# Attention megakernel: weighted sums taken two key tiles at a time, and the buffers regrouped for it

## The reference

```python
def ffn(x):                       # per sequence, N = 8 adapters, rank 64
    base = x @ W_base + b_base
    h = relu(x @ W_enc[n] + b_enc[n])                 # all n
    losses = mean((h @ W_dec[n] + b_dec[n] - x) ** 2) # one number per n
    a = connected_idx[argmin(losses)]
    return base + relu(x @ W_down[a] + b_down[a]) @ W_up[a] + b_up[a]

def attn(x):                      # 16 heads of 16, rotary q and k
    q, k, v = rope(x @ Wq + bq), rope(x @ Wk + bk), x @ Wv + bv
    return concat(softmax(q @ k.T / 4) @ v) @ W0 + b0

x = x + 0.5 * ffn(layernorm(x))
x = x + attn(layernorm(x))
x = x + 0.5 * ffn(layernorm(x))
```

## Time and profile before

| | before |
|---|---|
| time, median of 3 runs | 1844.04 us (1842.85 to 1847.05) |
| profiled execution: time, span of its instructions | 1842.72 us, 1840.9 us |
| PE busy | 1739.8 us, 95% |
| DVE busy | 1286.3 us, 70% |
| ACT busy | 978.3 us, 53% |
| POOL busy | 497.6 us, 27% |
| chain of work that ended last | PE 81%, DVE 11%, ACT 2%, DMA 2% |
| granted TensorE clock, mean | 0.976 of full speed |

### The profile page before, as it was taken

The page is one execution under the profiler, slowest core; times in us unless marked ns, Lnnn a source line. Parts: engine busy times, 40 slices in busy tenths (PEclk is TensorE's granted clock), DMA queues, the critical chain, the costliest instruction groups (busy, mean ns, idle before and its releaser), DMA issues.

```text
span 1840.9 us, 26466 instructions
## 1 busy us (share of the span) xinstructions
PE 1739.8 (95%) x9128; PEld 987.3 (54%) x9128; DVE 1286.3 (70%) x2795; ACT 978.3 (53%) x1954; POOL 497.6 (27%) x665
## 2 busy tenths in 40 slices
PE   6478999999999999999999999999999999999976
PEld 4343555555555555555556555555556555554434
DVE  5459686867768676776868677686867768686521
ACT  1126465655646565564646556474655637465531
POOL 2415041231414123141413214050322405032101
PEclk9689999999999999999999999999999999999996
DMA  4334231233333123333322333332233333214000
GB/s 117 58 59 79 43 52 37 45 69 58 70 58 53 38 41 67 58 70 58 58 36 51 54 59 69 58 61 39 52 46 58 70 58 61 46 41 69 18 12 12
DMA packets 96715, 99.38 MB, mean 54 GB/s; under 512 B 19972, under 2 KB 88261, under 8 KB 96453
## 3 DMA queue, kind: packets, MB, share of 16 engines
q1 hardware_dynamic: 93830, 97.16, 29.9%
q10 hardware_dynamic: 2752, 0.54, 0.2%
HBM read 63.54 MB, written 33.55 MB: 53 GB/s over the span
## 4 chain that ended last, share of the span: by engine, by line
PE 81%; DVE 11%; issue 2%; ACT 2%; DMA 2%; POOL 1%; SPq 0%; POOLq 0%; ACTq 0%; DVEq 0%
PE ps L725 11%; PE ps L784 10%; PE ps L737 10%; PE ps L713 10%; PE ps L800 10%; PE ps L802 6%; PE ps L842 5%; PE ps L858 4%; DVE mx L1088 4%; PE ps L843 3%; PE ps L824 3%; PE ps L868 2%; PE ps L769 2%; DVE xn L1119 2%; PE ps L889 1%
## 5 line engine op out<-in xcount | busy, mean ns | idle before, releaser
L1088 DVE TENSOR_REDUCE mx<-ps 128x1 f32<-128x512 f32 x1024 | 656.8, 683 | 287.2 <-PE ps L713 284.9
L940 ACT ACTIVATE pr<-ps 128x512 f32<-128x512 f32 x1024 | 556.2, 597 | 543.0 <-PE ps L725 541.9
L725 PE MATMUL ps<-stack 98*128 98x512 bf16 x1024 | 312.5, 384 | 7.9 <-ACT pr L940 2.4
L713 PE MATMUL ps<-stack 96*128 96x512 bf16 x1024 | 310.9, 381 | 4.7 <-DVE mx L1088 4.1
L737 PE MATMUL ps<-pr,va 128*32 128x512 f32 x2048 | 273.3, 604 | 1.2 <-ACT pr L940 1.1
L725 PEld LDWEIGHTS ps<-stack 98*128 98x128 bf16 x1024 | 73.9, 98 | 234.8 <-issue 158.1
L713 PEld LDWEIGHTS ps<-stack 96*128 96x128 bf16 x1024 | 99.0, 98 | 136.1 <-DVE mx L1088 30.6
L1315 POOL CAST wdh<-wd_all 128x128 fp32r x32 | 9.5, 296 | 555.9 <-DVE adapter L1169 499.9
L1141 DVE SCALAR_TENSOR_TENSOR ps<-ps,wb,h 128x512 f32<-128x512 f32 x128 | 96.8, 756 | 77.0 <-PE ps L802 76.9
L1250 POOL TENSOR_SCALAR rs<-mv 128x4 f32<-128x4 f32 x48 | 11.5, 239 | 471.6 <-DVE mv L1108 467.7
L1279 POOL TENSOR_TENSOR qb<-qb,cst 128x512 f32<-128x512 f32 x64 | 98.6, 1541 | 136.9 <-DVE qs L1195 136.9
(11 more groups left out here) (151 smaller groups left out, 2991.9 us busy)
## 6 DMA issues: line engine op xcount, KB each, us to landing
stack<-scratch SPq DMA_DIRECT2D x384, 128.0 KB, 6.1
scratch<-parts SPq DMA_DIRECT2D x64, 384.0 KB, 2.6
xin<-in_L_attn_x_dram SPq DMA_DIRECT2D x16, 512.0 KB, 4.4
out_dram<-x SPq DMA_DIRECT2D x16, 512.0 KB, 5.2
stack<-wu_mT SPq DMA_DIRECT2D x128, 4.0 KB, 1.7
cst<-in_const_dram SPq DMA_DIRECT2D x1, 1024.0 KB
raw<-in_L_ffn_W_dec_dram ACTq DMA_DIRECT2D x1, 512.0 KB, 5.6
pr<-in_L_ffn_W_enc_dram SPq DMA_DIRECT2D x2, 256.0 KB, 7.7
```

Of the source, the lines that this page charges most:

```text
L713: pe.matmul(bank1[:, t % 2, :], stack[0][0:KB, hd, 128 * t:128 * t + 128], stack[1][0:KB, hd, :], start=True, stop=True).then_inc(s1_full. ...
L725: pe.matmul(bank2[:, a % 2, :], stack[1][:, 4 * g + a, 128 * t:128 * t + 128], stack[0][:, 4 * g + a, :], start=True, stop=True).then_inc( ...
L940: act.activation(pr[:, n % 2, a, :], bank2[:, a % 2, :], ACT.Exp, scale=SCALE).then_inc(ex_done.sem, 1)
L1088: dve.tensor_reduce(mx[:, hd // 4 % 2, e:e + 1], bank1[:, t % 2, :], AX.X, ALU.max).then_inc(mx_done.sem, 1)
```

## The change

1. `pv` takes two key tiles in one stage: stage m does n = 2m and 2m + 1, 16 records in a row, and signals once. The tables list 8 of them per batch, at or near the place where the odd one of each two stood; the even ones go. `pr` gets a third part, and the tile of batch b and number n is `(16 b + n) % 3`, by the new function `held`. ACT waits for stage `(n - 3) // 2`.
2. `mt` transposes a full 128 columns of a new tile `mx_id`, which holds the two groups of maxima at both ends and the bf16 identity between them; the result lies in partitions 0 to 31 or 96 to 127. Before, it transposed 32 columns.
3. `cost` is one matmul in place of two. DVE now adds the two terms first, in the stage `gr` part 3, and waits there for the offsets that POOL computes.
4. To make room, the squares go into `xl` (float32r) before the low part is written there, so the low part waits for the squares (`xT_done`) in place of `xh_done`; and the normalised inputs `xn[2]` share memory with `xn[0]`, with two waits for the transposes that read them.

```diff
+        def held(b, n):
+
+            return pr[:, (b.number * G * T + n) % 3]
...
-            def pv(b, n):
-
-                g, t = divmod(n, T)
-                if n == 0:
+            def pv(b, m):
+
+                g = 2 * m // T
+                if m == 0:
                     pe.wait_ge(*va_done.at(b, 1))
-                if t == 0:
+                if 2 * m % T == 0:
                     pe.wait_ge(*raw_done.at(b, g - 1))
-                pe.wait_ge(*ex_done.at(b, 4 * n + 3))
-                for a in range(4):
-                    last = pe.matmul(bank_o[32 * a:32 * a + 32, :], va[b.odd][:, t, 4 * g + a, :], pr[:, n % 2, a, :],
-                                     start=(t == 0), stop=(t == T - 1))
+                pe.wait_ge(*ex_done.at(b, 8 * m + 7))
+                for n in (2 * m, 2 * m + 1):
+                    t = n % T
+                    for a in range(4):
+                        last = pe.matmul(bank_o[32 * a:32 * a + 32, :], va[b.odd][:, t, 4 * g + a, :], held(b, n)[:, a, :],
+                                         start=(t == 0), stop=(t == T - 1))
...
-                pe.transpose(bank[0:32, 0:64].bitcast(BF16), mx2[:, g % 2, :, :].rearrange("p a b -> p (a b)"),
-                             ident_b[:]).then_inc(mt_full.sem, 1)
+                pe.transpose(bank[:, 0:64].bitcast(BF16), mx_id[:, 64 * (g % 2):64 * (g % 2) + 128], ident_b).then_inc(mt_full.sem, 1)
...
-                pe.wait_ge(*z_step[f].at(b, 4))
                 pe.wait_ge(*zm_done[f].at(b, 0))
-                pe.matmul(bank[0:32, 0:N], ones, zt[f][:, 0, :], start=True, stop=False)
-                pe.matmul(bank[0:32, 0:N], ones, z[f][:], start=False, stop=True).then_inc(cost_full[f].sem, 1)
+                pe.matmul(bank[0:32, 0:N], ones, z[f][:], start=True, stop=True).then_inc(cost_full[f].sem, 1)
...
                 if half == 0:
-                    act.wait_ge(*pv_done.at(b, n - 2))
+                    act.wait_ge(*pv_done.at(b, (n - 3) // 2))
...
-                    act.activation(squares[:, s, c, :], bank, ACT.Square, accum_out=sxx[s][:, c:c + 1]).then_inc(xT_done[s].sem, 1)
+                    act.activation(xl[s][:, c, :], bank, ACT.Square, accum_out=sxx[s][:, c:c + 1]).then_inc(xT_done[s].sem, 1)
...
+                    dve.wait_ge(*z_step[f].at(b, 4))
+                    dve.sem_inc(passed, 1)
+                    dve.wait_ge(*zr_done[f].at(b, 0))
+                    dve.tensor_tensor(z[f][:], z[f][:], zt[f][:, 0, :], ALU.add).then_inc(zm_done[f].sem, 1)
```

More of the change, by code:

```diff
@@ L116, in tensor_order @@
     stage("s1", 0, 1, 0)
-    stage("pv", -1, 11)
+    stage("pv", -1, 5)
     stage("s2", -1, 12, 1)
@@ L133, in tensor_order @@
     stage("gr", +1, 0, 3)
-    stage("pv", -1, 13)
+    stage("pv", -1, 6)
     stage("s2", -1, 15, 0)
@@ L142, in tensor_order @@
     stage("up", -2, 1, 0)
-    stage("pv", -1, 15)
+    stage("pv", -1, 7)
     stage("s2", 0, 0, 0)
@@ L163, in tensor_order @@
     stage("ot", -1)
-    stage("pv", 0, 1)
+    stage("pv", 0, 0)
     stage("s2", 0, 2, 1)
@@ L177, in tensor_order @@
     stage("s2", 0, 4, 0)
-    stage("pv", 0, 3)
+    stage("pv", 0, 1)
     stage("s1", 0, 9, 0)
@@ L197, in tensor_order @@
     stage("s1", 0, 11, 1)
-    stage("pv", 0, 5)
+    stage("pv", 0, 2)
     stage("qk", +1, 2)
@@ L211, in tensor_order @@
     stage("en", -1, 1, 3)
-    stage("pv", 0, 7)
+    stage("pv", 0, 3)
     stage("s2", 0, 8, 1)
@@ L227, in tensor_order @@
     stage("gr", -1, 1, 3)
-    stage("pv", 0, 9)
+    stage("pv", 0, 4)
     stage("s2", 0, 10, 1)
@@ L499, in macaron @@
         x2 = sb("x2", [128, T, D])
-        xn = [sb(f"xn{s}", [128, T, D]) for s in range(3)]
+        xn = [sb(f"xn{s}", [128, T, D]) for s in range(2)]
+        xn.append(xn[0])
         whole = sb("whole", [128, C, S])
-        squares = sb("squares", [128, 2, C, S], BF16)
         xh, xl = ([sb(f"{n}{f}", [128, C, S], FR) for f in range(2)] for n in ("xh", "xl"))
@@ L529, in macaron @@
         mx = sb("mx", [128, 2, 4 * T])
-        mx2 = sb("mx2", [128, 2, 2, 4 * T], BF16)
-        pr = sb("pr", [128, 2, 4, S])
+        mx_id = sb("mx_id", [128, 128 + 64], BF16)
+        ident_b = mx_id[:, 32:160]
+        mx2 = [mx_id[:, 160 * o:160 * o + 32].rearrange("p (a b) -> p a b", a=2) for o in range(2)]
+        pr = sb("pr", [128, 3, 4, S])
         w_e = pr[:, 0, 0:2, :].rearrange("p c (n r) -> p c n r", r=R)
@@ L584, in macaron @@
         z_step = [sig(f"z_step{f}", 5) for f in range(2)]
+        zr_done = [sig(f"zr_done{f}", 1) for f in range(2)]
         zm_done = [sig(f"zm_done{f}", 1) for f in range(2)]
@@ L956, in maxima @@
                 act.wait_ge(*mq_done[g % 2].at(b, g // 2 - 1))
-                act.copy(mT[:, g % 2, :], bank[0:32, 0:64].bitcast(BF16)).then_inc(mT_done.sem, 1)
+                act.copy(mT[:, g % 2, :], bank[96 * (g % 2):96 * (g % 2) + 32, 0:64].bitcast(BF16)).then_inc(mT_done.sem, 1)
             def normalise(b, s, half):
@@ L977, in transposed @@
                     act.activation(whole[:, c, :], bank, ACT.Identity, accum_out=sx[s][:, c:c + 1])
-                    act.copy(xh[s][:, c, :], bank).then_inc(xh_done[s].sem, 1)
-                    act.activation(squares[:, s, c, :], bank, ACT.Square, accum_out=sxx[s][:, c:c + 1]).then_inc(xT_done[s].sem, 1)
+                    act.copy(xh[s][:, c, :], bank)
+                    act.activation(xl[s][:, c, :], bank, ACT.Square, accum_out=sxx[s][:, c:c + 1]).then_inc(xT_done[s].sem, 1)
                 else:
@@ L1134, in gram @@
             def gram(b, f, p):
+                bank = dense_bank(b, f, p)
                 if initial(b) and f == 0 and p == 0:
                     decoder_weights()
-                if p == 0:
-                    dve.wait_ge(*zm_done[f].at(b - 1, 0))
-                bank = dense_bank(b, f, p)
                 dve.wait_ge(*gr_full[f].at(b, p))
@@ L1207, in natural @@
                     dve.wait_ge(*oT_done.at(b - 1, C - 1))
-                    if not final(b):
-                        dve.wait_ge(*tr_full[2].at(b + 1, C - 1))
+                    dve.wait_ge(*tr_full[0].at(at_most_last(b + 2), C - 1))
                 dve.wait_ge(*nt_full.at(b, t))
```

38 lines of the change are left out of this document (15 added, 23 removed).

## The result

The changed kernel takes 1866.82 us (median of 4 runs, 1863.29 to 1870.43), the kernel before 1844.44 (4 runs, 1842.85 to 1847.05): 1.012 times as long, 95% interval 1.0097 to 1.0143. The forecast was 1860, with its own range 1850 to 1870 and a wider one of 1840 to 1874. The profiled execution took 1867.46 us.

A forecast was written before the change was run, and what follows sets the result against it. TensorE's own work was taken to bound the kernel, savings lasting until its next wait. 1842.7 us profiled, plus 13.5 (0.9 a batch, about 15 batches) and 3.5 for the ends, gave 1859.7: forecast 1860, range 1850 to 1870.

The forecast's parts named there:

- What a step costs: TensorE's `pv` stages: a lone one costs 1.10 us, a second in the same stage 0.91, so joining saves 0.19.
- Transposes and costs: Transposes of maxima at groups 1 and 3 and the cost matmuls: cheaper forms save 0.4 and 0.1 us a batch.
- Places 1 to 6: Six spots in one loop turn where TensorE gains or waits: sum +1.0 us per batch, taken as 0.9.
- place 6: Gram of feed-forward 1: without `pv` 8 TensorE waits for DVE's reading of the bank; +0.9 us a batch.
- Place 2: Cost of feed-forward 0: TensorE now arrives too early for exponentials and reductions; waits 0.35, saved 0.03, +0.3 us.
- The rest of the change: Shared `xn`, third part of `pr`, squares and low part in mid-run: no time lost in the turn.
- The ends: Start and end of the run: late low parts and DVE's added operation cost 2 to 5 us in all, taken 3.5.
- the 3.5 for the rest of the change: Amount added once for both ends: low parts behind the squares, plus DVE's added operation at the end.
- the late low part: At start and end, low parts wait for the squares with nothing beside them: 0.5 to 0.7 us each.
- the third rival: The DMA of the maxima becomes the wait, 0.3 to 0.5 us each batch: 1865 to 1872 us; chance 0.09.
- the savings do not arrive: Denies the first rival: waits at places 3 to 6 shrink, 1813 us with none, 1834 with half; chance 0.14.
- a plain count of -1.9: TensorE work saved per batch, in us, before any new waits; 30 us in all.

The follow-up runs named there:

- single `pv` stages: The changed kernel without the pairing, every `pv` tile a stage of its own at its old place: 1845.88 us, ratio 1.0003 to the kernel before.
- single-pair variants: Four kernels, each the changed one with one pair taken apart: 8, 9 (1856.59 us); 6, 7 (1859.47); 2, 3 (1858.35); 14, 15 (1866.80).

## Why the prediction was right, and which term was too small

- *What bounds*: TensorE, and a saving lasts until its next wait. Right; the experiments with pairs undone each removed the wait that the prediction names and gave part or all of that place's loss back.
- *What a step costs*: 1.10 for a single was right as a price; the second step is 0.86, not 0.91, because four groups in a row stand 0.43 apart and not 0.455. Over eight pairs that is 0.4 us a turn too much, more than the 0.1 to 0.2 by which the turn came out shorter than forecast.
- *Transposes and costs*, 0.5 a batch: right in the changed kernel (0.47), worth nothing with single `pv` stages.
- *Places 1 to 6*: sizes right within 0.25 (place 6, +0.65 for +0.9, is the furthest off), the sum 0.7 to 0.8 for 0.9. Place 2 was exact as a sum, but taken alone its pair costs only 0.10, for what is lost there is partly caught up later.
- *The rest of the change* at nothing in the turn: right (106.58 against 106.55).
- *The ends*: the term that was mis-sized, 17.9 us for 6.2. "In the last turn much waits already and a doubled `pv` only comes later" is what failed. Where TensorE has slack, a single `pv` stage fills a wait and costs nothing, and a pair pays its second step in full, as one place behind batch 15's scores shows (2.3 us); beside the single stages the pairs cost 6.3 us in the first two turns and 6.1 from batch 15's scores on. Of the 3.5 for the rest of the change, the late low part was sized rightly at the end (the last encoder waits 4.06 instead of 3.46 us, and the cost 1.31 instead of 1.20) and is nothing at the start, where the first encoder waits 5.16 us in both traces and not 0.5 to 0.7 more. Yet that rest costs 5.2 us at the end, with 10 us more at half clock: of the clock the prediction said nothing.
- *The total* fell into the range by two errors that partly cancel, the middle 3.9 us too dear and the ends 11.7 too cheap. At 1866.82 the number alone would suit the third rival (1865 to 1872) as well as the forecast; only the waits tell them apart.
- *Rivals*: the savings do not arrive, the waits do not shrink, and the DMA of the maxima is no wait of every batch. It comes three times in all (4.9 us; twice and 1.9 before), at 196, 1691 and 1782 us, in the second turn and behind batch 15's first scores.

In the first turn the longest new wait is 2.69 us for the exponentials, at 184.1 us, where the kernel before had 0.34 at 181.0. Why single-pair variants differ so much in the first two turns (289.9 to 295.3 us) was not taken further apart, nor which part of the rest of the change brings the half clock at the end, nor why three turns of the kernel before were longer.

## What to carry to other kernels

A saved instruction on the bounding engine is worth its price only up to the next awaited result, so sum a reordering place by place: here that came out at +0.7 to +0.8 against a plain count of -1.9. Size the first and last passes of a pipelined loop apart from the middle: with less work beside, what filled a wait there is paid in full once it is moved. And look at the granted clock at the ends, where cheap filler matmuls in unavoidable waits gave 0.8% to 1.1%, more than any order did (0.3%).

## What the runs showed of the hardware, unexpected

- One round trip into the 128x32 form and out costs 0.23 us, and inside it groups of four matmuls start 0.45 us apart at first, then 0.43.
- TensorE's granted clock fell to half at 1690.8 us, behind a wait of 1.38 us and two of 0.2 just ahead of it; where it stood at half behind a wait of 2.2 us, the `pv` pair took 1.3 longer (3.19 for 1.86).
- 224 extra matmuls of 512 columns within waits cost nothing that can be seen: the kernel with them is 14.6 us faster.
